# Momentum and its row sums ahead of the query gates, and the next chunk's key and query product behind the first square

## The chip, the cores and the metric

The kernel runs on one core of one Trainium2 chip. The metric is the device time of one execution in microseconds (us). Times of single instructions, waits and stretches come from one profiled execution.

## What is computed

The input x is 2048 rows of 256 values. After a layer norm two branches are added to it. One branch is a mixture of experts (32 routed experts, 8 of them per row from 2 of 4 groups, and one shared expert). The other is an attention block with a windowed softmax attention and a "fast weight" layer, a scan over 16 chunks of 128 rows, in which each chunk needs the weights that the chunk before it left:

```python
def step(carry, xi):
    W0, W1, W2, M0, M1, M2 = carry
    qi, ki, vi, l0, l1, l2, mi = xi
    hid  = q W2;  gate = silu(q W0);  out = (gate * hid) W1       # query side
    gba = k W0;   hbm = k W2;  sg = silu(gba);  dhidden = v W1    # key side
    dw0, dw1, dw2 = gradients(...)
    dw0 = dw0 + M0 * mean(mi)          # the same for dw1, dw2: the new momentum
    dw0 = newtonschulz5(dw0)           # X / norm(X), then 5 x: A = XX'; B = bA + cAA; X = aX + BX
    W0 = renorm(W0 + dw0, n0)
```

There are 4 heads of 64; the kernel holds them as two groups of two heads.

## The kernel before

There is one instruction list for each engine, written out by hand, and the engines meet at semaphores. The scan is `body(i, last)`, once per chunk i = 0 to 15, in each engine's list. An engine's list is executed in order, so the place of a call in `body` is the place of its instructions in the queue.

A chunk goes as follows. `k_side` makes the key-side products (TensorE L896) and VectorE forms the gradients' factors from them, ending with `dga` (L1355). `q_side` makes the query products into the PSUM bank M0; VectorE's `q_gate` (L1456) turns them into `gh` in two steps (L1459, L1461), and M0 is free again after that. `grads` on TensorE (L905) makes the gradients of each group into PSUM. `grad` on VectorE (L1367) adds the momentum (L1372), squares it (L1376) and sums the rows (L1379). `sums` on TensorE (L916) adds these row sums over the partitions, `sum_copy` on VectorE (L1381) copies the result out of PSUM, GpSimd takes the square root (`ss_pow`, L485), and `x_first` (L1385) scales the momentum to X.

Then come 20 Newton-Schulz stages, `st` = 0 to 19: five rounds of turn (`ns_turn`), Gram product (`ns_gram`), square (`ns_square`) and apply (`ns_apply`) on TensorE, for group 0 and then group 1. VectorE makes Am (L1410) after the Gram product and Mp (L1416) after the square; ScalarE copies XT after the turn and X after the apply. A dictionary `fill` in each `body` says what else the engine does after which stage: the query output (`q_out`, after stage 2), the attention, the preparation of the next chunk m = i + 1 (`prep_v` after stage 4, and so on).

The experts' work is cut into units that are placed in eight slots of each chunk, `h_slot(i, k)` and `y_slot(i, k)`. From slot 35 on the units are routed rows, so chunks 5 to 13 all have one in each slot, and the chunks before and after have fewer or shared-expert ones. `h_slot` makes the first product into bank HB, ScalarE applies relu and square (tile hb), VectorE multiplies by the gate weights (`h_weight`, L1689, instruction L1700), and `y_slot` makes the second product into bank YB. `y_slot(i, 1)` reads what `h_weight(i - 1, 7)` wrote. A queue of routing steps on VectorE is taken off one by one in the stages of chunk 1 and after.

The product of the next chunk's normalized input with the key and query weights has two halves on TensorE: `prep_qk(m)` (L861), which waits until `q_gate(i)` is done with M0, and `prep_qk_more(m)` (L866). Both halves are `M<-wall` in the profile, 128x512, each in two passes. ScalarE reads the result in its own `prep_qk` after stage 4 (L763). A small helper, `mm` at L829, issues all products, so nearly all have that line.

Of the kernel before, what the change touches and what calls it, by code (L numbers as in the profile page):

```python
# [86 lines left out]
def build(nc, x, wall_d, rows_d, wo, fast_d, affine_d, fc1T, fc2T, e1T, e2T, upT, downT, ident_d, fixed_d, out):  # L87
# [10 lines left out]
    with ExitStack() as ctx:  # L98
# [204 lines left out]
        def turned(t):  # L303

            return 1 if t == 0 else 2 + (t - 1) // 2
# [511 lines left out]
        def _(pe):  # L817
# [43 lines left out]
            def prep_qk(m):  # L861
                pe.wait_ge(e_xnT, turned(m))
                pe.wait_ge(e_gh, m)
                mm(M0[:, :], xnT_all[:, m, 0, :], wall[:, 0, 0:2 * D], True, False)

            def prep_qk_more(m):  # L866
                for k in range(1, KT):
                    ins = mm(M0[:, :], xnT_all[:, m, k, :], wall[:, k, 0:2 * D], False, k == KT - 1)
                ins.then_inc(e_pqa, 1)
# [106 lines left out]
            def q_out(i):  # L976
                pe.wait_ge(e_gh, i + 1)
                pe.wait_ge(e_aT, i + 1)
                for g in range(G):
                    ins = mm(M1[:, g * P:(g + 1) * P], gh[:, g, :], WT[g][:, W1, :])  # L980
                ins.then_inc(e_qo, 1)
# [147 lines left out]
            def body(i, last):  # L1129
                if last:  # L1130
                    q_side(i)
                    att_turn(i)
                    q_out(i)
                    att_scores(i, True)
                    last_turn(6)
                    last_fc2(6)
                    att_turn_p(i, True)
                    att_pv(i)
                    last_turn(7)
                    last_fc2(7)  # L1140
                    turn_comb(i)
                    out_wo(i)
                    return
                m = i + 1
                k_side(i, 0)
                k_side(i, 1)
                q_side(i)
                att_turn(i)
                y_slot(i, 0)
                grads(i, 0)  # L1150
                grads(i, 1)
                h_slot(i, 0)
                prep_qk(m)
                sums(i, 0)
                sums(i, 1)
                prep_qk_more(m)
                y_slot(i, 1)
                fill = {2: [lambda: q_out(i)], 3: [lambda: h_slot(i, 2)], 4: [lambda: prep_v(m)],
                        5: [lambda: y_slot(i, 3)], 6: [lambda: h_slot(i, 3)], 8: [lambda: prep_mom(m)],
                        9: [lambda: prep_turn_v(m), lambda: y_slot(i, 4)], 10: [lambda: h_slot(i, 4)],  # L1160
                        11: [lambda: att_scores(i, False)], 12: [lambda: prep_turn_qk(m)],
                        13: [lambda: y_slot(i, 5)], 14: [lambda: h_slot(i, 5)],
                        15: [lambda: att_turn_p(i, False)], 16: [lambda: att_pv(i)]}
                if i == SORT_STEP:
                    fill[11] = [prefixes] + fill[11]
                if i == LAST - 1:
                    for n, st in ((0, 3), (1, 7), (2, 11), (3, 15)):
                        fill[st] = fill.get(st, []) + [lambda n=n: last_turn(n)]
                    for n, st in ((0, 6), (1, 10), (2, 14), (3, 18)):
                        fill[st] = fill.get(st, []) + [lambda n=n: last_fc2(n)]  # L1170
                for st in range(4 * NI):
                    for g in range(G):
                        if st % 4 == 0:
                            ns_turn(g, st // 4 == NI - 1)
                            if st == 0 and g == 0:
                                h_slot(i, 1)
                        elif st % 4 == 1:
                            ns_gram(g, st // 4)
                            if st == 1 and g == 0:
                                y_slot(i, 2)  # L1180
                        elif st % 4 == 2:
                            ns_square(g)
                        else:
                            ns_apply(g, st // 4)
                    for f in fill.get(st, []):
                        f()
                y_slot(i, 6)
                turn_comb(i)
                h_slot(i, 6)
                if i == LAST - 1:  # L1190
                    last_turn(4)
                    last_fc2(4)
                out_wo(i)
                y_slot(i, 7)
                h_slot(i, 7)
                if i == LAST - 1:
                    last_turn(5)
                    last_fc2(5)
                turn_w(m, 0)
                turn_w(m, 1)  # L1200
# [14 lines left out]
            for i in range(1, LAST):  # L1215
                body(i, False)
# [4 lines left out]
        def _(dve):  # L1221
# [510 lines left out]
            def body(i, last):  # L1732
                if last:
                    q_gate(i)
                    att_scale(i)
                    last_sum(6)
                    q_ms(i)
                    att_mask(i)
                    att_max(i)
                    last_sum(7)  # L1740
                    last_out(6)
                    q_norm(i)
                    att_out(i)
                    total(i)
                    last_out(7)
                    return
                m = i + 1
                k_side(i)
                if i:
                    h_weight(i - 1, PER - 1)  # L1750
                q_gate(i)
                grad(i)
                sum_copy(i, 0)
                sum_copy(i, 1)
                h_weight(i, 0)
                x_first(i)
                shared_add(i, 0)
                fill = {0: [lambda: shared_add(i, 1), lambda: att_scale(i)], 2: [lambda: h_weight(i, 1), lambda: shared_add(i, 2)],
                        3: [lambda: q_ms(i)], 5: [lambda: q_norm(i), lambda: prep_silu_qk(m)],
                        6: [lambda: h_weight(i, 2), lambda: prep_z(m), lambda: shared_add(i, 3)],  # L1760
                        7: [lambda: prep_silu_v(m)], 8: [lambda: prep_ss8(m)],
                        9: [lambda: h_weight(i, 3), lambda: prep_mean(m)],
                        10: [lambda: lr_a(m), lambda: prep_qkn(m), lambda: shared_add(i, 4)],
                        12: [lambda: att_mask(i)], 13: [lambda: att_max(i)],
                        14: [lambda: lr_b(m), lambda: shared_add(i, 5)], 15: [lambda: h_weight(i, 4)], 16: [lambda: lr_c(m)],
                        17: [lambda: att_out(i)], 18: [lambda: h_weight(i, 5)]}
                if i == LAST - 1:
                    for n, st in ((0, 0), (1, 5), (2, 9), (3, 13)):
                        fill[st] = fill.get(st, []) + [lambda n=n: last_sum(n)]
                    for n, st in ((0, 8), (1, 12), (2, 16), (3, 18)):  # L1770
                        fill[st] = fill.get(st, []) + [lambda n=n: last_out(n)]
                if i == 0:
                    for n, st in ((5, 0), (6, 2), (7, 4), (8, 6)):
                        fill[st] = fill.get(st, []) + [lambda n=n: ln_stats(n)]
                    for n, st in ((5, 2), (6, 4), (7, 6), (8, 8)):
                        fill[st] = [lambda n=n: ln_shift(n)] + fill.get(st, [])
                for st in range(4 * NI):
                    for g in range(G):
                        if st % 4 in (1, 2):
                            (ns_a, ns_m)[st % 4 - 1](i, g, st // 4)  # L1780
                        if st == 4 * NI - 1:
                            update(i, g)
                        if routing and (i, st) >= (SORT_STEP, 1) and (g or i > SORT_STEP):
                            routing.pop(0)()
                    for f in fill.get(st, []):
                        f()
                if i == LAST - 1:
                    last_sum(4)
                shared_add(i, 6)
                renorm(m)  # L1790
                w_bd(m)
                if i == LAST - 1:
                    last_sum(5)
                    last_out(4)
                total(i)
                shared_add(i, 7)
                h_weight(i, 6)
                if i == LAST - 1:
                    last_out(5)
# [75 lines left out]
```

## Time and profile before

| what | value |
|---|---|
| median of 3 runs | 770.02 us (770.01 to 770.32) |
| the profiled execution, its time | 768.66 us |
| its span | 766.8 us |
| granted TensorE clock, mean | 0.967 of full |

The span is the time from the first to the last instruction of the profile. In the rows, PE is TensorE's products, PEld its weight loads, DVE is VectorE, ACT ScalarE, POOL GpSimd. "CC<-r,fixed" says that tile CC was written from tiles r and fixed, with buffer numbers left out. "x2" after a row merges two instructions: the time is from the start of the first to the end of the second.

### The profile page before, as it was taken

To read this page: it belongs to the slowest core of one execution; us is meant where nothing else is said; L and a number is where in the kernel's file an instruction comes from. 1 tells how busy PE (TensorE), PEld (TensorE's weight loads), DVE (VectorE), ACT (ScalarE), POOL (GpSimd) and SP (SyncE) were. 2 spreads that over 40 slices of the span, in tenths; PEclk is the share of its full clock that TensorE was granted. 3 is DMA by queue.
4 is the path that set the end of the run, shared out by engine and by line. 5 is a ranking of instruction groups with operands and counts; after the bars stand their busy time and mean duration, and the time that the engine had idled before them with its cause. 6 is when DMAs were issued, how large, how long until landed. Compare 5 with 4: busy or idle time off the path is not lost.

```text
span 766.8 us, 22396 instructions
## 1 busy us (share of the span) xinstructions
PE 663.5 (87%) x8887; PEld 549.8 (72%) x8887; DVE 544.9 (71%) x1893; ACT 403.6 (53%) x1061; POOL 238.9 (31%) x299
## 2 busy tenths in 40 slices
PE   3788678989998989898998999989999898987875
PEld 2666467777776777777888777877877777765653
DVE  5866886576565686777968778786776867757664
ACT  3575343452553646656476464755657466452542
POOL 2422122055654031322313132131320313267640
PEclk9799979999999999999999999999999999998897
DMA  8300000140101244453453535435454442010220
GB/s 276 121 2 2 1 3 1 27 159 23 34 24 50 69 140 137 147 180 121 152 163 110 181 119 173 161 109 163 135 177 160 145 139 91 12 33 27 62 74 28
DMA packets 40152, 75.38 MB, mean 98 GB/s; under 512 B 9712, under 2 KB 24432, under 8 KB 40048
## 3 DMA queue, kind: packets, MB, share of 16 engines
q1 hardware_dynamic: 36224, 68.08, 27.5%
q0 software_dynamic: 2048, 4.33, 1.8%
q10 hardware_dynamic: 1776, 1.54, 0.6%
q8 instruction: 71, 1.16, 0.6%
q14 instruction: 33, 0.27, 0.1%
HBM read 64.73 MB, written 9.20 MB: 96 GB/s over the span
## 4 chain that ended last, share of the span: by engine, by line
PE 58%; DVE 22%; ACT 12%; issue 5%; DMA 1%; POOL 1%; SPq 0%; ACTq 0%; DVEq 0%; POOLq 0%
PE CC L829 17%; PE YB L829 13%; PE HB L829 12%; PE M L829 10%; ACT hb L563 3%; DVE Am L1410 3%; DVE hb L1700 2%; ACT WT L563 2%; PE CC L922 1%; ACT XT L563 1%; PE M L1011 1%; ACT prT L563 1%; DVE Mom L1372 1%; DVE Mp L1416 1%; DMA rows<-in_rows 1%
## 5 line engine op out<-in xcount | busy, mean ns | idle before, releaser
L421 POOL TENSOR_TENSOR r<-r,half 128x3 f32<-128x3 f32 (+1 forms) x78 | 81.7, 1053 | 197.7 <-DVE r L1287 102.6
L1410 DVE TENSOR_TENSOR Am<-CC,shifts 128x192 f32<-128x192 f32 x150 | 48.0, 352 | 82.5 <-PE CC L829 82.5
L563 ACT ACTIVATE hb<-HB 128x512 f32<-128x512 f32 x86 | 51.3, 597 | 80.4 <-PE HB L829 80.0
L563 ACT ACTIVATE XT<-CC 128x256 f32<-128x256 f32 x150 | 50.7, 381 | 71.4 <-PE CC L923 71.2
L829 PE MATMUL HB<-xsT,e_s 128*128 128x128 f32 x560 | 79.4, 286 | 0.0
L829 PE MATMUL YB<-e_s,hb 128*128 128x128 f32 x560 | 77.5, 282 | 0.0
L1700 DVE TENSOR_TENSOR hb<-hb,cwb 128x512 f32<-128x512 f32 x70 | 76.8, 1097 | 0.0
L829 PE MATMUL CC<-X,Mp 64*64 64x64 f32 x1800 | 57.1, 235 | 21.0 <-DVE Mp L1416 20.9
L829 PEld LDWEIGHTS YB<-e_s,hb 128*128 128x128 f32 x560 | 69.3, 191 | 7.1 <-issue 4.3
L829 PEld LDWEIGHTS HB<-xsT,e_s 128*128 128x128 f32 x560 | 68.7, 193 | 3.0
L829 PEld LDWEIGHTS CC<-X,Mp 64*64 64x64 f32 x1800 | 46.6, 138 | 31.8 <-DVE Mp L1416 25.3
L563 ACT ACTIVATE X<-CC 128x192 f32<-128x192 f32 x150 | 43.7, 333 | 45.7 <-PE CC L829 45.1
L829 PE MATMUL CC<-Am 64*64 64x64 f32 x1800 | 57.1, 235 | 12.0 <-DVE Am L1410 11.7
L829 PE MATMUL CC<-XT 64*64 64x64 f32 x1800 | 56.7, 235 | 8.3 <-ACT XT L563 7.9
L829 PEld LDWEIGHTS CC<-XT 64*64 64x64 f32 x1800 | 44.4, 135 | 25.6 <-ACT XT L563 17.0
L829 PEld LDWEIGHTS CC<-Am 64*64 64x64 f32 x1800 | 44.6, 136 | 24.5 <-DVE Am L1410 18.5
L829 PE MATMUL M<-wall,xnT_all 128*128 128x512 f32 (+1 forms) x128 | 54.0, 528 | 2.1 <-DMA rows<-in_rows 1.2
L1416 DVE SCALAR_TENSOR_TENSOR Mp<-CC,rests 128x192 f32<-128x192 f32 x150 | 47.8, 350 | 11.2 <-PE CC L829 10.6
L563 ACT ACTIVATE hb<-hb 128x512 f32<-128x512 f32 x86 | 54.2, 630 | 1.3
L922 PE MATMUL CC<-ident,X 128*64 128x128 f32 x150 | 39.8, 286 | 11.4 <-ACT X L563 7.0
L421 POOL TENSOR_TENSOR r<-r,neghalf 128x4 f32<-128x4 f32 x16 | 16.2, 1014 | 100.9 <-DVE r L1467 100.9
L470 POOL COPY akT<-akT 128x256 f32<-128x256 f32 x16 | 6.3, 397 | 118.9 <-issue 118.9
(229 smaller groups left out, 1513.3 us busy)
## 6 DMA issues: line engine op xcount, KB each, us to landing
e_s<-in_e1T SPq DMA_DIRECT2D x35, 512.0 KB, 4.6
e_s<-in_e2T SPq DMA_DIRECT2D x35, 512.0 KB, 5.7
cwb<-tile_weights SPq DMA_DIRECT2D x35, 512.0 KB, 3.7
sorted_rows<-e_s SPq DMA_DIRECT2D x5, 476.0 KB, 10.1
xs<-sorted_rows SPq DMA_DIRECT2D x35, 68.0 KB, 5.2
sorted_out<-yo SPq DMA_DIRECT2D x35, 64.0 KB, 2.8
out<-xnT_all SPq DMA_DIRECT2D x8, 256.0 KB, 2.1
x_all<-in_x SPq DMA_DIRECT2D x1, 1408.0 KB, 15.5
```

What stands on the lines that cost most here:

```text
L421: return pool.tensor_tensor(dst, src, expo[:, 0:n], ALU.pow)
L470: pool.tensor_copy(akT[:, :, 0, :], akT[:, :, 1, :])
L563: return nc.scalar.activation(out_, in_, func, **kw)
L829: return pe.matmul(out_, lhsT, rhs, start=start, stop=stop)
L922: pe.transpose(CA[g][0:HD, 0:P], X[g][:, 0, :], ident[:, :])
L1011: ins = pe.transpose(M1[:, n * P:(n + 1) * P], pr[:, h, w, :], ident[:, :])
L1372: nc.vector.scalar_tensor_tensor(Mom[g][:, :, :].rearrange(flat), Mom[g][:, :, :].rearrange(flat), mmc[:, g:g + 1], CA[g][:, 0:3 * HD], AL ...
L1410: nc.vector.tensor_tensor(Am[g][:, :, :], PROD[g], shifts[:, it, :].unsqueeze(1).to_broadcast([P, 3, HD]), ALU.add)\
L1416: nc.vector.scalar_tensor_tensor(Mp[g][:, :, :], PROD[g], NS[it][2], rests[:, it, :].unsqueeze(1).to_broadcast([P, 3, HD]), ALU.mult, ALU. ...
L1700: nc.vector.tensor_tensor(hb[u % RING][:, :, :], hb[u % RING][:, :, :], gate, ALU.mult).then_inc(e_hw, 1)
```

## The change

On TensorE the two halves of the next chunk's key and query product leave their places around `sums` and stand together behind stage 2 (the first square of both groups), after `q_out`. On VectorE `grad(i)` stands ahead of the last expert weighting of the chunk before and of the query gates.

```diff
@@ TensorE, body
                 grads(i, 0)
                 grads(i, 1)
                 h_slot(i, 0)
-                prep_qk(m)
                 sums(i, 0)
                 sums(i, 1)
-                prep_qk_more(m)
                 y_slot(i, 1)
-                fill = {2: [lambda: q_out(i)], 3: [lambda: h_slot(i, 2)], 4: [lambda: prep_v(m)],
+                fill = {2: [lambda: q_out(i), lambda: prep_qk(m), lambda: prep_qk_more(m)], 3: [lambda: h_slot(i, 2)], 4: [lambda: prep_v(m)],
@@ VectorE, body
                 m = i + 1
                 k_side(i)
+                grad(i)
                 if i:
                     h_weight(i - 1, PER - 1)
                 q_gate(i)
-                grad(i)
                 sum_copy(i, 0)
                 sum_copy(i, 1)
                 h_weight(i, 0)
```

## Rows read from the trace of the kernel before

**Rows 1.** The page: its span and TensorE's busy time.

```profile
span 766.8 us, 22396 instructions
PE 663.5 (87%) x8887; PEld 549.8 (72%) x8887; DVE 544.9 (71%) x1893; ACT 403.6 (53%) x1061; POOL 238.9 (31%) x299
```

**Rows 2.** Chunks 5 to 12: stretch; length; PE, PEld, DVE, ACT, POOL busy; PEclk; DMA.

```profile
281.80:654.40 372.60, 344.35 (x4870) 294.00 (x4870) 283.53 (x865) 222.52 (x585) 89.57 (x112) 1.00 0.46 146
```

**Rows 3.** Timeline of chunk 7, VectorE: start, duration, instruction, [idle before].

```profile
374.97 0.28 DVE L1355 TENSOR_TENSOR dga<-kt 128x128 f32<-128x128 f32 x1
...
375.17 1.08 DVE L1700 TENSOR_TENSOR hb<-hb,cwb 128x512 f32<-128x512 f32 x1
...
376.17 0.41 DVE L1459 TENSOR_TENSOR gt<-M,gsig 128x256 f32<-128x256 f32 x1
376.62 0.42 DVE L1461 TENSOR_TENSOR gh<-M,gt 128x256 f32<-128x256 f32 x1
376.96 0.73 DVE L1372 SCALAR_TENSOR_TENSOR Mom<-Mom,mmc,CC 128x192 f32<-128x192 f32 x2
...
378.14 0.61 DVE L1379 TENSOR_REDUCE r<-sq 128x3 f32<-128x192 f32 x2
...
378.97 0.42 DVE L1383 COPY r<-CC 128x3 f32<-128x3 f32 x2 [0.22 <-PE CC L829]
...
379.30 1.08 DVE L1700 TENSOR_TENSOR hb<-hb,cwb 128x512 f32<-128x512 f32 x1
```

**Rows 4.** Timeline of chunk 7, TensorE.

```profile
375.75 0.28 PE L829 MATMUL CC<-hid,vl 128*64 128x64 f32 x2
...
377.19 1.10 PE L829 MATMUL M<-wall,xnT_all 128*128 128x512 f32 x2
...
378.54 0.65 PE L829 MATMUL CC<-r,fixed 128*128 128x3 f32 x4 [0.26 <-DVE r L1379]
...
379.05 1.10 PE L829 MATMUL M<-wall,xnT_all 128*128 128x512 f32 x2
...
379.99 1.05 PE L829 MATMUL YB<-e_s,hb 128*128 128x128 f32 x8
...
381.12 0.30 PE L922 MATMUL CC<-ident,X 128*64 128x128 f32 x1
```

**Rows 5.** The chain that ended last, chunk 7, behind the first Gram product.

```profile
385.06 0.45 PE CC L829 x12
385.51 0.64 PE M L829 x4
386.15 0.61 PE CC L829 x22
386.76 1.10 PE HB L829 x8
```

**Rows 6.** Timeline of chunk 3: half a product, the sums, the copy, the turn.

```profile
187.56 1.02 PE L829 MATMUL M<-wall,xnT_all 128*128 128x512 f32 x2
...
188.42 0.50 PE L829 MATMUL CC<-r,fixed 128*128 128x3 f32 x4
188.74 0.38 DVE L1383 COPY r<-CC 128x3 f32<-128x3 f32 x2 [1.28 <-PE CC L829]
...
191.46 0.27 PE L922 MATMUL CC<-ident,X 128*64 128x128 f32 x1
```

**Rows 7.** The chain that ended last, chunk 1, then chunk 4.

```profile
89.31 0.52 DVE Am L1410 x2
...
246.85 0.28 ACT tsq L563
```

**Rows 8.** Busy time and granted clock by stretch, three of them.

```profile
252.50:255.90 3.40, 2.33 (x49) 1.71 (x45) 1.23 (x4) 2.87 (x10) 0.21 (x1) 1.00 0.53 167
255.90:259.30 3.40, 3.37 (x44) 3.03 (x48) 3.16 (x10) 1.50 (x2) 1.43 (x1) 0.52 0.06 13
706.50:713.30 6.80, 6.30 (x85) 5.22 (x85) 3.89 (x12) 2.15 (x7) 4.40 (x5) 0.51 0.13 39
```

## The prediction

> **What bounds the kernel now.** I began with the page: TensorE is busy 87% of the span and VectorE 71% [rows 1]. An average over stages says little here, so I cut the span at the last k-side product of each chunk (dga, L1355). Eight chunks in the middle take 372.6 us, 46.6 us each, TensorE busy 344.4 of it at full clock [rows 2]; they repeat so exactly that one, chunk 7, can stand for the nine chunks 5 to 13. Per chunk TensorE is idle (372.6 - 344.4) / 8 = 3.5 us only.
>
> Then the timeline of chunk 7, once for VectorE and once for TensorE. From dga (374.97) to the first Newton-Schulz turn (381.12) VectorE works without a break but for 0.22 us: expert weighting, two gate steps, momentum, squares, row sums, copy, the next expert weighting, X [rows 3]. TensorE follows it: gradients end at 375.75 + 0.28 = 376.03, the products of chunk 8 (M<-wall) are slipped in before and after the sums, the expert outputs (YB) end at 381.04, and the turn starts at 381.12 [rows 4]. So the stretch is VectorE's, and TensorE fills it almost wholly. After it the chain of waits turns over: from the squares at 385.06 through q_out, apply and the expert product to 387.86 each piece is TensorE's and each begins as the one ahead ends [rows 5]. There any new TensorE work is paid in full.
>
> **Part one: the order on VectorE.** Nothing is added; six instructions (Mom, sq, r for both groups) go ahead of the 1.00 us weighting and the two gate steps. What do they wait for? Mom of group 1 needs the group 1 gradients, 376.03, so it starts at 376.07; now it starts as the second of the pair at 376.96 + 0.73 - 0.41 (one gate step, as wide a bound for one Mom as these rows have) = 377.28 [rows 3, 4]. The row sums so come some 1.22 us earlier, ending at 377.53 in place of 378.14 + 0.61 = 378.75. But the copy of the sums out of PSUM (sum_copy) stands behind weighting and gates in the new order. These take 376.96 - 375.17 = 1.79 us, from 377.45 on (one starts 0.08 before the other ends): the copy starts at 377.45 + 1.79 = 379.24. It starts at 378.97 now. The early row sums therefore win nothing: **+0.27 us**, which is the old wait of 0.22 saved and about 0.5 of waiting for gradients added. Behind the copy stand the weighting of the next unit and X; GpSimd's powers run beside that weighting and move with the copy. X and the first turn are +0.27, at 381.39.
>
> Who else waits? The expert outputs (YB) need the late weighting, done at 377.45 + 1.08 = 378.53 in place of 376.25; TensorE, done with the sums by then, makes them in 1.05 us, to about 379.6, long before 381.39: no cost. The next gate output is late by 2.3 us (379.33), but q_out reads it at 385.5 and the moved product at 386: no cost. SyncE's expert loads wait for the YB end, which comes 1.4 us sooner: no cost; DMA issues none new.
>
> **Part two: the product of the next keys and queries.** Two halves, each one 128x512 product in two passes. Half of it costs 188.42 - 187.56 = 0.86 us of TensorE [rows 6], the whole 1.72. It leaves the stretch before the turn, where it costs nothing today in chunks 5 to 13 (VectorE sets the end), and goes between q_out and apply. There Mp of both groups is ready when q_out ends at 386.15, so apply, the expert product, and behind them relu, square and XT on ScalarE all move by the whole: **+1.72 us** [rows 5]. Its readers on ScalarE stand in stage 4, one stage on, so they don't wait.
>
> Per chunk 5 to 13: 0.27 + 1.72 = 1.99, nine times: 17.9 us.
>
> **The other chunks.** Without the late weighting the same shift is about +0.25. Chunk 0: 0.25 + 1.72 = 2.0. Chunk 1: VectorE's routing work keeps Am waiting until 89.31 anyway, which hides some 0.6; ScalarE's copies after q_out, now beside the product, hide 0.3 [rows 7]: 1.1. Chunks 2, 3, 4: here the sums wait on TensorE behind the shared expert's product and half of the moved one; the copy waits 1.28 to 1.5 us for it [rows 6]. With that half gone the copy starts 0.7 sooner (then the gates hold it). Chunk 2: 1.72 - 0.7 = 1.0. Chunk 4: less another 0.3 for those copies, 0.7. Chunk 3: the turn at 191.46 waits on TensorE's queue, which loses 1.72 but then meets X, for a gain of 1.5: 0.2. Chunk 14: its stages run at a granted clock of 0.51 until 713.3 [rows 8], so part of the product costs double: 0.3 + 1.7 + 1.0 = 3.0. Together 8.0.
>
> **Sum.** 17.9 + 8.0 = 25.9. The profiled execution took 768.66 us with a span of 766.8, 1.4 below the median of the three runs, 770.02; the shift is taken against the median: 770.0 + 25.9 = 795.9, say **796**.
>
> Unknown costs. How far a later idle gap takes up the product: at most 1.72, at least 0; I take 0 taken up, since the rows nearest (the chain of chunk 7) have no gap. What the new gap on TensorE (about 379.6 to 381.4, and 0.6 before it) does to its clock: at least 0. The record shows the clock falling to 0.52 for 3.4 us right behind a stretch in which TensorE was busy 2.33 of 3.40 us [rows 8]; a fall with all of it on the path costs half of 3.4, 1.7. I take 0 for the likeliest, since chunks 5 to 12 are idle 3.5 us each and kept 1.00 throughout [rows 2], and keep 1.7 for the range. The Trainium skill (TensorE: Matmul & The Clock Gate, Part 1) says that TensorE runs at 1.2 GHz when idle and at 2.4 GHz when busy: if the new gap passes for idle there, the time is that of the first rival below, if not, that of the sum; rows 8 agree with its two rates.
>
> **Rivals.** First, **the clock**: the product kept TensorE busy just where it waits for X. With it gone the stretch from 377.9 to 381.4 holds about 1.1 us of work; if the clock falls behind it in 4 to 7 of the 13 chunks that have the gap, at 1.7 us each, the time is 802.5 to 807.6, say 805. For: the fall after 252.5 to 255.9 [rows 8]. Against: the idle time that cost no clock [rows 2].
>
> Second, **half of the product is absorbed**: 3.5 us idle per chunk exist [rows 2], most of them waits for VectorE and ScalarE later in the stages. If the other engines use the 1.72 us to catch up and half of it is given back in 15 chunks, that is 12.9 less: 783. Against: those waits are for work that itself follows the delayed TensorE.
>
> Third, **not slower**: the product fits wholly in an idle gap behind the first square, because apply waits there for Mp of group 1 anyway. Then only the VectorE shift is left: twelve chunks by +0.27 is 3.2, chunks 2 to 4 give back 0.7 + 1.5 + 0.7 = 2.9: 770.3; if the freed TensorE also brings the turn forward by a little, 767. It decides from the point where apply would wait 1.72 us for Mp. Against: it waits for nothing at 386.15 [rows 5].
>
> That the change doesn't do what it says is part of my main case: the row sums are early, the copy of them is not.
>
> **How the numbers follow.** Main case 0.55 (792 to 800), clock 0.27 (800 to 810), half absorbed 0.12 (780 to 790), not slower 0.06 (766 to 772). Leaving out the last, the top of the clock case and the bottom of the half absorbed one gives 786 to 808. A measurement of this kernel can tell some 0.2% (1.5 us). Only the last case isn't slower by more: faster 0.03, same 0.03, slower 0.94.
>
> **What would show it.** In the changed profile, chunks 5 to 13 should take 48.6 us, 2.0 more. The row sums should end about 2.6 us behind dga's start (now 3.8), followed by weighting and gates without idle time, and the copy 4.3 behind dga (now 4.0). TensorE should show a gap of about 1.7 us before the first turn, and between q_out and apply four wall products in 1.7 us. A granted clock under 1.00 over chunks 5 to 13 is the first rival. Wrong I am if the stretch from the squares to XT grows by much less than 1.7, or if the turn comes earlier after dga than 6.15 us.

## The result, and the profile after

| | before | after |
|---|---|---|
| median | 770.01 us (767.25 to 770.32) | 823.69 us (819.64 to 824.09) |
| span of the profiled execution | 766.8 us | 821.8 us |
| granted TensorE clock, mean | 0.967 | 0.926 |

The ratio is 1.069, with a 95% interval of 1.067 to 1.071. The change makes the kernel 53.7 us slower. The forecast was 796 with a range of 786 to 808: the direction was right, the size half of the measured one, and the range missed.

The page of the changed kernel (its parts 1, 2 and 4), which answers to [rows 1]:

```profile
span 821.8 us, 22396 instructions
PE 687.1 (84%) x8887; PEld 568.6 (69%) x8887; DVE 546.6 (67%) x1893; ACT 405.6 (49%) x1061; POOL 245.6 (30%) x299
...
PEclk9899678999999989989899998998999989899888
...
PE 65%; DVE 17%; ACT 9%; issue 4%; POOL 3%; DMA 1%; SPq 0%; ACTq 0%; DVEq 0%; POOLq 0%
```

The number of instructions is the same, but TensorE is busy 23.6 us longer with them. That points to a slower rate, and the clock row (in tenths of full speed) shows an 8 every few slices throughout the middle.

Busy time by stretch in the changed kernel: chunks 5 to 12 from dga to dga, which answers to [rows 2], and then, in chunk 7, TensorE's gap ahead of the first turn and the stretch behind it:

```profile
291.50:702.14 410.64, 360.79 (x4872) 308.59 (x4870) 284.92 (x866) 223.45 (x585) 94.48 (x112) 0.94 0.42 133
397.90:401.98 4.08, 1.18 (x10) 0.97 (x9) 3.18 (x10) 0.46 (x1) 2.51 (x2) 0.76 0.75 249
402.00:408.60 6.60, 6.37 (x70) 5.50 (x70) 2.93 (x10) 2.33 (x6) 0.00 (x0) 0.63 0.31 88
```

A chunk now takes 410.64 / 8 = 51.33 us, 4.76 more than the 46.57 of before; eight chunks give 38.0 of the 53.7 us. TensorE is busy 1.18 of 4.08 us in the stretch that ends with the first turn, and behind it runs at a mean granted clock of 0.63, that is for most of the time at the lower of its two levels (1.2 GHz). The same stretch of the kernel before, and then the time at the lower level in the changed one:

```profile
377.90:381.10 3.20, 2.88 (x15) 1.83 (x14) 2.78 (x10) 0.52 (x1) 1.89 (x2) 1.00 0.91 255
400.02:406.85 6.83, 4.87 (x31) 4.38 (x32) 3.42 (x12) 1.89 (x4) 1.91 (x2) 0.50 0.43 138
```

The clock falls at 400.0, when TensorE has been idle for only 0.3 us (its expert outputs end at 399.70), and comes back at 406.9. The turn is at 401.98, so some 2 of the 6.8 us at the lower level pass in the idle gap and cost nothing.

The timeline of chunk 7, VectorE, GpSimd and TensorE, which answers to [rows 3, 4] (lines behind the first edit are numbered two lower than before):

```profile
394.91 0.28 DVE L1353 TENSOR_TENSOR dga<-kt 128x128 f32<-128x128 f32 x1
...
396.01 0.41 DVE L1370 SCALAR_TENSOR_TENSOR Mom<-Mom,mmc,CC 128x192 f32<-128x192 f32 x1 [0.17 <-PE CC L829]
...
396.88 0.61 DVE L1377 TENSOR_REDUCE r<-sq 128x3 f32<-128x192 f32 x2
...
397.28 0.64 PE L829 MATMUL CC<-r,fixed 128*128 128x3 f32 x4 [0.22 <-DVE r L1377]
397.40 1.08 DVE L1698 TENSOR_TENSOR hb<-hb,cwb 128x512 f32<-128x512 f32 x1
...
398.54 1.16 PE L829 MATMUL YB<-e_s,hb 128*128 128x128 f32 x8 [0.61 <-DVE hb L1698]
398.85 0.42 DVE L1459 TENSOR_TENSOR gh<-M,gt 128x256 f32<-128x256 f32 x1
399.19 0.22 DVE L1381 COPY r<-CC 128x3 f32<-128x3 f32 x2
399.33 1.07 DVE L1698 TENSOR_TENSOR hb<-hb,cwb 128x512 f32<-128x512 f32 x1
399.42 2.51 POOL L421 TENSOR_TENSOR r<-r,half 128x3 f32<-128x3 f32 x2 [5.79 <-DVE r L1381]
...
401.98 0.42 PE L922 MATMUL CC<-ident,X 128*64 128x128 f32 x1 [2.29 <-DVE X L1391]
...
402.41 1.91 PE L829 MATMUL HB<-xsT,e_s 128*128 128x128 f32 x8
```

The row sums end 397.49, 2.58 us behind dga's start, as forecast (2.6). The copy starts 4.28 behind it, as forecast (4.3). The turn doesn't: 7.07 us behind dga, where 6.15 was before and 6.42 forecast. Between copy and turn stands GpSimd, with 2.51 us for two square roots. In the kernel before the same pair takes 1.89:

```profile
379.21 1.89 POOL L421 TENSOR_TENSOR r<-r,half 128x3 f32<-128x3 f32 x2 [5.53 <-DVE r L1383]
```

And the expert product behind the turn takes 1.91 us for its eight pieces, where at the full clock such a product takes 1.06 to 1.16.

The chain that ended last, chunk 7, which answers to [rows 5]:

```profile
408.13 0.45 PE CC L829 x12
408.58 2.36 PE M L829 x8
410.94 0.61 PE CC L829 x22
411.55 1.10 PE HB L829 x8
```

q_out and the moved product stand as one piece of 2.36 us where q_out alone had 0.64: + 1.72, all on the path.

### The profile page after: what moved, and what is told of

Read it like the earlier page. It is cut to its first block, busy times and chain, and to the rows that moved or that the text cites. A ratio compares the mean times of both kernels' runs of the same rounds, so it can differ in the third digit from the quotient of the medians.

```text
span 821.8 us, 22396 instructions
## 1 busy us (share of the span) xinstructions
PE 687.1 (84%) x8887; PEld 568.6 (69%) x8887; DVE 546.6 (67%) x1893; ACT 405.6 (49%) x1061; POOL 245.6 (30%) x299
## 3 DMA queue, kind: packets, MB, share of 16 engines
q8 instruction: 71, 1.16, 0.6%
## 4 chain that ended last, share of the span: by engine, by line
PE 65%; DVE 17%; ACT 9%; issue 4%; POOL 3%; DMA 1%; SPq 0%; ACTq 0%; DVEq 0%; POOLq 0%
PE CC L829 19%; PE YB L829 14%; PE M L829 13%; PE HB L829 11%; POOL r L421 3%; ACT hb L563 2%; DVE Am L1408 2%; PE CC L922 2%; ACT WT L563 1%; PE CC L923 1%; DVE hb L1698 1%; PE M L1011 1%; ACT XT L563 1%; DMA rows<-in_rows 1%; ACT prT L563 1%
## 5 line engine op out<-in xcount | busy, mean ns | idle before, releaser
L421 POOL TENSOR_TENSOR r<-r,half 128x3 f32<-128x3 f32 (+1 forms) x78 | 87.2, 1124 | 222.8 <-DVE r L1285 128.4
L829 PE MATMUL YB<-e_s,hb 128*128 128x128 f32 x560 | 85.3, 299 | 5.5 <-DVE hb L1698 5.5
L829 PE MATMUL HB<-xsT,e_s 128*128 128x128 f32 x560 | 83.6, 295 | 0.0
L829 PEld LDWEIGHTS YB<-e_s,hb 128*128 128x128 f32 x560 | 74.9, 206 | 9.5 <-DVE hb L1698 6.3
L829 PEld LDWEIGHTS HB<-xsT,e_s 128*128 128x128 f32 x560 | 73.0, 203 | 3.0
L922 PE MATMUL CC<-ident,X 128*64 128x128 f32 x150 | 42.7, 305 | 36.2 <-DVE X L1391 29.2
L829 PE MATMUL CC<-XT 64*64 64x64 f32 x1800 | 59.7, 243 | 7.7 <-ACT XT L563 7.5
L829 PEld LDWEIGHTS CC<-XT 64*64 64x64 f32 x1800 | 46.9, 142 | 27.0 <-ACT XT L563 16.3
L1414 DVE SCALAR_TENSOR_TENSOR Mp<-CC,rests 128x192 f32<-128x192 f32 x150 | 47.8, 350 | 11.2 <-PE CC L829 10.6
L829 PE MATMUL M<-wall,xnT_all 128*128 128x512 f32 (+1 forms) x128 | 51.5, 528 | 2.1 <-DMA rows<-in_rows 2.1
L922 PEld LDWEIGHTS CC<-ident,X 128*64 128x64 f32 x150 | 17.7, 118 | 45.5 <-DVE X L1391 33.3
```

The lines of the kernel that those rows point to most:

```text
L421: return pool.tensor_tensor(dst, src, expo[:, 0:n], ALU.pow)
L829: return pe.matmul(out_, lhsT, rhs, start=start, stop=stop)
L922: pe.transpose(CA[g][0:HD, 0:P], X[g][:, 0, :], ident[:, :])
L1414: nc.vector.scalar_tensor_tensor(Mp[g][:, :, :], PROD[g], NS[it][2], rests[:, it, :].unsqueeze(1).to_broadcast([P, 3, HD]), ALU.mult, ALU. ...
```

## The experiments

The theory after the result: the 4.76 us per chunk are three things, the product (1.72), the late turn (0.92) and TensorE's lower clock from the emptied stretch on (the rest). The rivals say that the clock is beside the point, or that only one half of the change is to blame.

**Each half alone, and the product by itself.** First the product's move alone, with VectorE's order of before:

```diff
@@ TensorE, body, against the kernel before
-                prep_qk(m)
                 sums(i, 0)
                 sums(i, 1)
-                prep_qk_more(m)
...
-                fill = {2: [lambda: q_out(i)], ...
+                fill = {2: [lambda: q_out(i), lambda: prep_qk(m), lambda: prep_qk_more(m)], ...
```

> Only TensorE's half of the change: the two halves of the next product go behind the first square, VectorE's order stays as before. Theory (clock): the product's 1.72 us per chunk come on the path, and the stretch ahead of the first turn has about 2.3 us of idle TensorE per chunk in place of almost none, so the granted clock falls behind it as in the changed kernel; only the 0.9 us by which the first turn comes late in chunks 5 to 13 are missing, 9 x 0.9 = 8. So about 814 us, mean clock 0.93. Rival (VectorE's new order is what makes the clock fall, by its longer gap): no fall, 770 + 15 x 1.7 = 796 us, mean clock 0.96 or more.

Measured: 804.78 us, ratio 1.045 (1.042 to 1.048), mean clock 0.937. It lies between the two. The clock does fall without VectorE's half, so the rival is out; but it falls less than I expected: in six of chunks 5 to 12, in two of them for 6.8 us and in four for 3.4 (the trace read in stretches of 0.2 us), while the changed kernel has a fall in all eight, six of them of 6.8 us. Where it doesn't fall, in chunks 8 and 9, a chunk takes 48.28 us.

Then the product twice, at its old places unused and behind the first square for use. The unused one has no `then_inc`:

```diff
@@ TensorE, body, against the kernel before
                 prep_qk(m)
                 sums(i, 0)
                 sums(i, 1)
-                prep_qk_more(m)
+                prep_qk_more(m, False)
...
-                fill = {2: [lambda: q_out(i)], ...
+                fill = {2: [lambda: q_out(i), lambda: prep_qk(m), lambda: prep_qk_more(m)], ...
```

> VectorE's order as before. The product is made at its old places around the sums, where its result is not used, and once more behind the first square, where it counts. Theory (clock): TensorE is as busy ahead of the first turn as before, so the clock holds (0.96) and the product costs only its own time on the path, 15 x 1.7 = 26 us less a little: 792 to 797 us, chunks 5 to 13 at 48.3 us each. Rival (the place behind the square is itself worse than its own time, for what is queued behind it): over 805 us, with the clock at 0.96.

Measured: 795.35 us, ratio 1.034 (1.032 to 1.036), 25.6 us over the 769.7 of the kernel before beside it, with a mean clock of 0.968. Chunks 5 to 12, busy time by stretch:

```profile
291.48:677.82 386.34, 357.98 (x4904) 298.70 (x4902) 283.78 (x865) 223.63 (x585) 87.67 (x112) 1.00 0.44 141
```

48.29 us per chunk: 1.72 more than before, to the hundredth what the rows of before gave for the product. It also shows that the work ahead of the turn was free: the product's move alone, without that work, takes the same 48.28 where the clock holds. The product's move alone costs 804.8 and this one 795.4, though this one does more. In chunks 5 to 12 it is 396.5 us against 386.3, and there the difference is the clock's; the other chunks weren't taken apart.

VectorE's half alone needs one liberty: TensorE's product can't stay ahead of the sums, or it would hold them until the gates are done. It stays ahead of the first turn, but behind the sums:

```diff
@@ against the changed kernel: TensorE, body
                 sums(i, 0)
                 sums(i, 1)
-                y_slot(i, 1)
-                fill = {2: [lambda: q_out(i), lambda: prep_qk(m), lambda: prep_qk_more(m)], ...
+                if y_unit(i, 1)[1] == "rows":
+                    y_slot(i, 1)
+                    prep_qk(m)
+                    prep_qk_more(m)
+                else:
+                    prep_qk(m)
+                    prep_qk_more(m)
+                    y_slot(i, 1)
+                fill = {2: [lambda: q_out(i)], ...
```

> Only VectorE's half of the change. TensorE's product stays ahead of the first turn, but both halves behind the sums (with expert rows also behind the expert outputs), since ahead of the sums it would wait for the gates. Theory: the first turn is 0.92 us later in chunks 5 to 13, as in the changed kernel, 8 us, the other chunks gain a little from the sums that no longer wait for the product: 775 to 780 us with the clock at 0.96. Of the 0.92, 0.27 is the forecast's and 0.65 a longer square root on GpSimd (2.51 us for two in place of 1.89). Rival (the early row sums do pay once TensorE's part is out of the way): 770 us or less.

Measured: 778.48 us, ratio 1.012 (1.010 to 1.015), mean clock 0.972. Chunks 5 to 12:

```profile
281.52:661.34 379.82, 343.62 (x4872) 293.94 (x4870) 284.07 (x866) 222.51 (x585) 94.58 (x112) 1.00 0.45 143
```

47.48 us per chunk, 0.91 more. So VectorE's new order costs time by itself, with the clock at 1.00. TensorE's queue isn't quite that of before, but it doesn't hold the turn: in chunk 7 it is done 0.57 us ahead of it. The early row sums don't pay.

**The clock.** The changed kernel with an unused product put into TensorE's gap:

```diff
@@ TensorE, body, against the changed kernel
                 y_slot(i, 1)
+                prep_qk(m)
+                prep_qk_more(m, False)
                 fill = {2: [lambda: q_out(i), lambda: prep_qk(m), lambda: prep_qk_more(m)], ...
```

> The changed kernel, with one more product, whose result is not used, behind the sums and the expert outputs and ahead of the first turn, where TensorE is idle in the changed kernel. It adds 1.72 us of TensorE work per chunk. Theory (clock): the clock holds in most chunks, and the time falls to about 802 us (770, and per chunk 5 to 13 1.72 for the product and 0.92 for the late turn, and some 8 for the other chunks), mean clock 0.96. Rival (the fall of the clock is hidden beside other waits and the loss has another cause): 824 us or more, whatever the clock.

Measured: 799.75 us, ratio to before 1.039 (1.037 to 1.042), mean clock 0.971. More work, 23.9 us less time than the changed kernel. Chunks 5 to 12:

```profile
292.23:685.80 393.57, 357.37 (x4904) 298.71 (x4902) 284.18 (x865) 223.45 (x585) 93.61 (x112) 1.00 0.44 138
```

49.20 us per chunk at 1.00 in place of 51.33 at 0.94. The difference, 2.13, is the clock's share, and 49.20 - 46.57 = 2.63 is the sum of the two halves, 1.72 + 0.91. The three parts add up in these chunks.

Half of the spare product, and then, as a control, the same spare work at a place that is full already:

```diff
@@ TensorE, body, against the changed kernel: half a spare product in the gap
                 y_slot(i, 1)
+                pe.wait_ge(e_gh, i + 1)
+                mm(M0[:, :], xnT_all[:, i, 0, :], wall[:, 0, 0:2 * D])
                 fill = {2: [...
@@ the same, the control: the spare product behind the square
-                fill = {2: [lambda: q_out(i), lambda: prep_qk(m), lambda: prep_qk_more(m)], ...
+                fill = {2: [lambda: q_out(i), lambda: prep_qk(m), lambda: prep_qk_more(m, False),
+                            lambda: prep_qk(m), lambda: prep_qk_more(m)], ...
```

> The changed kernel with half of a product (128x512, 0.86 us), its result unused, in TensorE's gap ahead of the first turn. Theory (the clock falls because of the work that this gap has lost): half of it already keeps the clock in most chunks, 799 to 808 us, mean clock 0.95 or more, and chunks 5 to 12 at 49.2 us where it holds. Rival (only the whole product keeps it): 815 us or more.

Measured: 800.7 us, ratio 1.040 (1.037 to 1.043), mean clock 0.967.

```profile
290.77:684.36 393.59, 350.49 (x4888) 295.68 (x4886) 284.24 (x865) 223.57 (x585) 95.63 (x112) 1.00 0.43 138
```

The same 49.20 us per chunk: half the product in the gap is enough to keep 1.00 in these chunks.

> A control: the changed kernel with the same spare work of TensorE as the one with the spare product (1.72 us per chunk), but behind the first square, beside the product that counts, and not in the gap. Theory (the gap decides, not the amount of work in a chunk): the clock falls as in the changed kernel, 0.92 to 0.94, and the work costs its own time: 823.7 + 15 x 1.7 = 849 us, 843 to 853. Rival (more TensorE work anywhere keeps the clock up): 825 us, clock 0.96.

Measured: 850.32 us, ratio to before 1.104 (1.102 to 1.107), mean clock 0.931; 26.6 us over the changed kernel. It isn't the amount of TensorE work that keeps the clock, but that there be some in this gap.

**The late turn.** VectorE's half alone, with one expert weighting moved behind `x_first`:

```diff
@@ VectorE, body, against the kernel of VectorE's half alone
                 sum_copy(i, 1)
-                h_weight(i, 0)
                 x_first(i)
+                h_weight(i, 0)
```

> The kernel of only VectorE's half (778.5 us), with the expert weighting of slot 0 put behind x_first, so that VectorE waits while GpSimd takes the two square roots. Theory (the square root is longer there because the weighting, 128x512 from two operands, starts 0.1 us before it and holds GpSimd off until it ends): each root takes 0.84 us, the two 1.7 in place of 2.5, the first turn comes 0.8 us sooner per chunk in chunks 5 to 13, and the time is 771 to 773 us. Rival (the root is longer for another reason, such as waiting for the copy or for instructions): 2.5 us remain, and 778 us or more.

Measured: 771.92 us, ratio 1.004 (1.002 to 1.005). A chunk takes 46.74 us in place of 47.48. The roots and the weighting in the timeline of chunk 7:

```profile
380.89 0.22 DVE L1388 COPY r<-CC 128x3 f32<-128x3 f32 x2
381.12 1.67 POOL L421 TENSOR_TENSOR r<-r,half 128x3 f32<-128x3 f32 x2 [5.79 <-DVE r L1388]
...
383.51 1.09 DVE L1705 TENSOR_TENSOR hb<-hb,cwb 128x512 f32<-128x512 f32 x1
```

Two roots take 1.67 us once no weighting stands beside them, against 2.52 before that move. The move takes no wait away from GpSimd, only the weighting from beside it. In the changed kernel the weighting starts at 399.33 and the root at 399.42, and X of group 0 begins at 401.15, 0.75 behind the weighting's end: nearly the length of one root (0.84), as if it had begun shortly before the weighting ended. In the kernel before the root starts first, at 379.21, and the weighting at 379.30. So the order of these two starts, 0.09 us apart, goes with the length. No run changed the order alone, but the traces of all twelve kernels agree over chunks 5 to 13: 2.51 to 2.53 us wherever the weighting starts first, 1.89 to 1.94 wherever the root does, 1.67 where it comes behind X, or only once the second root has begun. It flipped because in the new order both sums are ready when the copies come, so the second copy follows at once (the pair takes 0.22 us, not 0.42) and the weighting is 0.1 us too early.

The Trainium skill (SBUF — State Buffer, section SBUF: two separate sides) has the rule: a VectorE instruction with two operands from SBUF and a GpSimd instruction that reads SBUF exclude each other, and whichever starts first holds the shared port pair for its whole length. The weighting reads hb and cwb from SBUF, the root r and half; the traces agree for a weighting that starts first, with 2.5 us against 1.67. For a root that starts first they don't: the weighting at 379.30 takes 1.08 us beside it, and 1.09 alone, so it was not held.

The same move in the changed kernel:

> The changed kernel with the same move. Theory: the turn comes 0.8 us sooner, 7 us over chunks 5 to 13, and TensorE's gap ahead of it is shorter by as much, so that the clock falls less often or for a shorter time as well: 810 to 817 us, mean clock 0.93 to 0.945. Rival (the fall of the clock doesn't depend on the length of this gap): 816 to 818 us with the clock at 0.926.

Measured: 797.82 us, ratio to before 1.036 (1.033 to 1.039), mean clock 0.954, well under what I expected. That is 25.9 us less than the changed kernel, where the roots explain 7. With the gap shorter by 0.8 us out of about 2.3, the clock falls in three of chunks 5 to 12 (5, 7 and 11), for 3.4 us each, in place of all eight: 48.89 us per chunk here, at 0.99.

```profile
288.95:680.10 391.15, 348.49 (x4872) 297.96 (x4870) 285.10 (x866) 223.60 (x585) 86.88 (x112) 0.99 0.43 139
```

But the length of this gap alone doesn't say how often the clock falls. The time from dga to the turn in chunk 7, with the product's move alone and then here:

```profile
394.08:400.24 6.16, 3.80 (x45) 3.35 (x42) 5.68 (x17) 1.52 (x4) 1.90 (x2) 0.95 0.86 257
386.93:393.15 6.22, 3.95 (x44) 3.42 (x41) 4.76 (x17) 1.53 (x4) 1.67 (x2) 1.00 0.78 257
```

TensorE does nearly the same amount of work in them. With the product's move alone the idle piece right ahead of the turn is even the shorter one, 0.94 against 1.44 us, and yet the clock falls in six chunks there and in three here. With half of a spare product that piece is 1.44 us as well, and the clock falls in none of the eight. What separates six from three isn't shown by these runs.

**Two kernels meant to be faster.** The same move in the kernel before, and then the change's aim carried through in chunks 5 to 12:

> The kernel before, with the same move of the weighting of slot 0 behind x_first and nothing else. Theory: two roots take 1.68 in place of 1.89 us, X comes 0.2 us sooner, the expert outputs of slot 2 wait for the weighting by nearly nothing: 766 to 769 us. Rival (the weighting, now late, holds the expert outputs of slot 2 and with them the second group's Gram product): 771 to 776 us.

Measured: 768.97 us, ratio 0.9989 (0.9972 to 1.0005), not to be told from no change. Per chunk 46.36 in place of 46.57: the 0.2 is there in the trace, and too small for the total.

```diff
@@ chunks 5 to 12, against the kernel before: VectorE, body
                     k_side(i)
+                    grad(i)
+                    sum_copy(i, 0)
+                    sum_copy(i, 1)
+                    q_gate(i)
                     h_weight(i - 1, PER - 1)
-                    q_gate(i)
-                    grad(i)
-                    sum_copy(i, 0)
-                    sum_copy(i, 1)
-                    h_weight(i, 0)
                     x_first(i)
+                    h_weight(i, 0)
@@ TensorE, body; y_slot(i, 1) takes the place of h_slot(i, 1) between the turns
                 h_slot(i, 0)
-                prep_qk(m)
                 sums(i, 0)
                 sums(i, 1)
+                h_slot(i, 1)
+                prep_qk(m)
                 prep_qk_more(m)
-                y_slot(i, 1)
```

> What the change seems to be after, in chunks 5 to 12 alone: momentum, row sums and also the copy of the sums ahead of the gates and of the late weighting; TensorE makes the sums, then the first product of slot 1, then the product of the next keys and queries, which stays ahead of the first turn, and the expert outputs between the two turns. Theory: the copy comes 1 us sooner, the roots run beside the gates, and the turn then waits for TensorE's own queue, about 0.4 us sooner than before: 8 x 0.4 = 3, so 765 to 769 us. Rival (the gates, now late, hold the product and with it the turn): 770 to 776 us.

Measured: 769.54 us, ratio 1.0002 (0.9989 to 1.0016). The chain of waits, chunk 7 of this kernel:

```profile
378.52 0.44 DVE gh L1466
378.96 0.14 issue
379.09 1.95 PE M L829 x4
381.05 0.11 PE CC L922
```

The mechanism works: with the copy ahead of the gates the roots start 1.2 us sooner, and X is no longer what the turn waits for. What it waits for is next in line: the product, which can't start before the gates. A chunk takes 46.35 us, 0.22 less where I expected 0.4, and the total, just above the range I gave, doesn't show it. None of the ten kernels beats the kernel before by more than its measurement is uncertain.

## Why the prediction was wrong in size

- **The product, right.** 1.72 us per chunk: measured 1.72 in chunks 5 to 12, and 25.6 over all fifteen (the product made twice). That nothing behind the square absorbs it, against the second rival, is shown by the same run.
- **The order of the row sums, right.** They come early and the copy doesn't, with both times as forecast.
- **The late turn, term mis-sized.** "X and the first turn are +0.27", "GpSimd's powers run beside that weighting and move with the copy": the turn is +0.92 late (7.07 - 6.15), chunks 5 to 12 cost 0.91 each in VectorE's half alone. The powers did move with the copy, but no longer ran beside the weighting: they waited behind it. My sum moved two engines by the same amount and didn't ask which of two instructions starts first where they had been 0.09 us apart.
- **The clock, the step that failed.** "I take 0 for the likeliest, since chunks 5 to 12 are idle 3.5 us each and kept 1.00 throughout." That compared idle time over a whole chunk, when it is the work lost at one place that counts: there TensorE had been busy 2.88 us of 3.2 before (377.9 to 381.1), and was now busy 1.18 of 4.08. The first rival named mechanism and place, and was underpriced twice. It gave 4 to 7 of 13 chunks; the granted clock fell in all eight of chunks 5 to 12, and in 13. It gave one fall of 3.4 us; in six of the eight the clock stayed low for 6.8 us, in two for 3.4. In all that is 47.8 us at half clock in chunks 5 to 12, and it costs 8 x 2.13 = 17.0 there, less than half of 47.8 because some of it passes in the idle gap. Over the whole kernel it costs 23.9 us (the changed kernel against that with the spare product). By its own terms the ends of that rival are 802.7 and 807.8, 0.2 over those written.
- **The two errors fed each other.** The late root made the gap 0.7 us longer than forecast. With the root back to its length in the changed kernel, the clock fell in three of the eight chunks and the total was 25.9 us less, of which the earlier turn itself is 7.
- **The other chunks.** With the spare product in the gap the whole is 30.0 us slower than before, of which chunks 5 to 13 at 2.63 make 23.7: some 6 are left for the others, where I had 8.0. From dga to dga, chunks 0 to 4 of the changed kernel take 1.7, 3.7, 1.8, 0.5 and 1.1 us more than before, where I had 2.0, 1.1, 1.0, 0.2 and 0.7. The term furthest off is chunk 1: its granted clock was 0.77 (79.26 to 131.50) in place of 0.86 (76.74 to 125.25). That the clock is its cause was not tried.

The sum with the measured terms: 26 for the product, 9 for the turn, 24 for the clock, less some 4 by which the two halves together (30.0, with the spare product) cost less than each by itself (25.6 + 8.8): 54, measured 53.7. That it closes is no test, since the 24 and the 30.0 are the two parts of the measured difference; the test is chunks 5 to 12, where 1.72 and 0.91 come from runs of their own and give the 2.63.

## What to carry to other kernels

Before taking TensorE work out of a wait, ask what else that work did there: it was free, and it kept the clock. If it must go, half of it left behind as unused work can be worth more than it costs, here 23 us. And when two engines meet within a tenth of a microsecond, price both orders of their starts; a reordering on one engine may flip them.

## What the runs showed of the hardware that was not expected

- A turn later by 0.84 us, and with it a longer gap of TensorE, changed the time by 26 us, of which 7 are the turn itself: the clock fell in all eight of chunks 5 to 12 in the changed kernel (0.94 over them), and in three with the weighting moved (0.99). A fall of 3.4 us cost such a chunk 1.3 to 1.5 us in these two kernels, one of 6.8 us 2.2 to 2.6.
- The clock fell before the long pause was over: in chunk 7 of the changed kernel 0.3 us into a pause of 2.29 us, with products between shorter pauses ahead of it. In chunks 8 and 11 it fell 1.2 us behind the turn.
- Adding 0.86 us of unused TensorE work per chunk made the kernel faster by 23 us, from 823.7 to 800.7.
- A VectorE instruction of 1.08 us that starts 0.09 us ahead of a GpSimd instruction delays it nearly to its own end: two square roots take 2.51 us, against 1.89 when GpSimd starts 0.09 us ahead, and 1.67 with no such instruction beside them. The VectorE instruction takes the same 1.08 us in both orders.
